# A decoder layer on one core: ScalarE normalises the attention's rows instead of VectorE, GpSimd makes the offsets, and the calls of all engines stand in another sequence

## The chip, the cores and the metric

The kernel runs on one core of a Trainium2 chip. A core has TensorE (PE, matrix products, with weight loads shown as PEld), VectorE (DVE), ScalarE (ACT, table functions and affine maps), GpSimd (POOL) and SyncE (SP), which here only issues transfers. Each engine works through its own list of instructions in order and waits at semaphores for the others. The metric is the device time of one execution in microseconds (us), lower is better.

## The reference, cut to what matters

```python
# x, ctx: (16, 256, 512); one decoder layer
Q = (LN(x) @ wq.T) in 16 heads of 32;  K, V = one shared head of 32, both squeezed to 8 and grown again
Q, K = rope(Q), rope(K);  K, V = quantise_8bit(K), quantise_8bit(V)      # over all 16 batches
for i in range(0, 256, 64):                                              # windows of 128 keys
    wout = (sigmoid(Qw Kw^T / sqrt(32)) / (row sum + 1e-8)) Vw           # blended where windows overlap
x1 = x + out @ wo.T
k  = LN(x1)                                                              # the step that is moved
x2 = x1 + wkv(w, u, k, ctx)                                              # a scan over 256 tokens
h  = silu(q(LN(x2)) @ tern(w_gate).T) * (q(LN(x2)) @ tern(w_up).T)
out = x2 + q(rms_norm(h) * ln_weight) @ tern(w_down).T                   # q: 8 bit per row, tern: -1, 0, 1
```

`LN` is `(x - mean) / sqrt(var + 1e-5)` over the 512 columns, without weights.

## The kernel before, in words

**Tiles.** A batch is 256 tokens by 512 columns: two halves `t` of 128 token rows (one per partition), or four chunks `c` of 128 columns. The hidden width 2048 is worked in four pieces `n` of 512. All arithmetic but the matrix products of the feed-forward part is fp32.

**Stages.** A long prologue brings in all of `x`, makes K and V of all batches, finds their common extrema and rounds the three weight matrices to -1, 0, 1. Then each batch passes through attention (`queries`, `rope`, `rotate`, `scores`, `probs`, `dens`, `nums`, `blend_windows`, `attention_out`, `residual`), the norm of its rows (`att_norm`), the scan (`key_steps`, `wkv_keys`, `exps`, `values`, `scan`, `join`, `outputs`, `quotient`, `wkv_back`, `wkv_residual`), quantisation (`wkv_norm`, `wkv_quantise`, `scale_tokens`, `wkv_round`) and the feed-forward part (`gate_up`, `silu`, `hidden`, `squares`, `weigh_hidden`, `peak`, `hidden_scale`, `scale_hidden`, `round_hidden`, `down`, `output`).

**What sets the order.** There is no scheduler. Each of the five engine programs is a list of calls written out by hand: a prologue, a loop `for i in range(4, B)` that is a software pipeline (batch `b = i` is in attention while `w = i-1` is in the scan and `f`, `g`, `h` = `i-2`, `i-3`, `i-4` are in the feed-forward part), and an epilogue. One pass of the loop is called a round here; it takes one batch in and one out. The lists differ in where a round is cut, which by itself means nothing: what counts is the sequence and the semaphores.

**The norm.** `residual` adds the attention's output to the rows of `x` and takes `bn_stats` of each half (L1425, L1427). `att_norm` (DVE) joins the statistics into mean and variance (L1376), waits for GpSimd's `att_rstd`, which adds epsilon and raises to the power -1/2 (L1805, L1807), and then subtracts the mean and multiplies by the inverse deviation in one `tensor_scalar` per half (L1381), from `x_rows` into `tok`. GpSimd's `key_steps` subtracts a table from `tok` (L1842), TensorE's `wkv_keys` transposes it (L618), ScalarE's `exps` (L1003) follows.

**The ways between the engines that the prediction walks.** `wkv_round` (L1504) writes the quantised tokens `q_tok`; SyncE's `turn_tokens` (L337) transposes them by a transfer into `qT`; TensorE's `gate_up` (L646) reads them and ScalarE's `silu` (L1012) reads its first result. `hidden_scale` (L1531 to L1537) releases `scale_hidden` (L986, the multiply) and `round_hidden` (L996, to bf16), two long ScalarE steps for each half of the hidden rows. `probs` (L947) is the sigmoid of the scores, sixteen pieces per batch, in four groups between which TensorE makes the next scores. `spin` (L658) is a run of products that nobody reads, put where TensorE would stand idle. Change of function set on ScalarE costs a load of its tables (rows with ACT_TABLE_LOAD): `silu`, `probs` and the logarithms and exponentials each need another set.

Of the kernel before, what the change touches and what calls it, by code (L numbers as in the profile page):

```python
# [13 lines left out]
P = 128  # L14
# [27 lines left out]
def build(nc, a, out, k_scratch, v_scratch):  # L42
# [10 lines left out]
    spare = sb("spare", [P, 1])  # L53
    warm = sb("warm", [P, 1])
# [155 lines left out]
    eps_set, win_set = event("eps_set", 6), event("win_set", 4)  # L210
# [29 lines left out]

    key_T, exp_set, value_set = event("key_T"), event("exp_set", NC), event("value_set")
# [24 lines left out]
    def sync_program(sy):  # L266
# [115 lines left out]
        load_x(0)  # L382
        load_small()
        load_x(1)
        load_columns(0)
        load_columns(2)
        load_columns(1)
        load_x(2)
        load_x(3)
        load_columns(3)  # L390
        load_x(4)
        load_columns(4)
        load_x(5)
        store_trig(1)
        load_columns(5)
        load_x(7)
        store_trig(0)
        load_columns(6)
        load_x(6)
        load_keys(0)  # L400
        load_wq()
        load_columns(7)
        load_weights(GATE, 1)
        load_weights(GATE, 0)
        load_queries(0)
        store_trig(5)
        load_weights(GATE, 2)
        next_residual(1)
        store_trig(2)
        load_weights(GATE, 3)  # L410
# [4 lines left out]
        next_keys(0)  # L415
        load_weights(UP, 2)
        load_weights(UP, 3)
        next_queries(0)
        next_residual(0)
        store_trig(3)  # L420
        load_weights(DOWN, 1)
        load_weights(DOWN, 0)
        turn_queries(1, 0)
        store_trig(4)
        load_weights(DOWN, 2)
        turn_queries(1, 1)
        store_trig(6)
        load_weights(DOWN, 3)
        store_trig(7)
        next_queries(1)  # L430
        next_keys(1)
        next_values(0)
        turn_tokens(0)
        turn_queries(2, 0)
        turn_queries(2, 1)
        next_queries(2)
        next_keys(2)
        next_values(1)
        turn_tokens(1)
        turn_hidden(0, 0, 0)  # L440
        turn_queries(3, 0)
        turn_queries(3, 1)
        turn_hidden(0, 0, 1)
        for i in range(4, B):
            b, w, f, g, h = i, i - 1, i - 2, i - 3, i - 4
            next_keys(w)
            next_queries(w)
            turn_hidden(h, 1, 0)
            turn_hidden(h, 1, 1)
            store(h, 1)  # L450
            store(h, 0)
            next_residual(f)
            next_values(f)
# [1329 lines left out]
    def pool_program(ge):  # L1783
# [35 lines left out]
        def att_rstd(b):  # L1819
            row_rstd("att", b, x1_mv, x1_var, x1_rstd)  # L1820
# [260 lines left out]
```

## Time and profile before

| | |
|---|---|
| median of 3 runs | 994.83 us (992.13 to 996.42) |
| the profiled execution's own time | 994.31 us |
| its span, first to last instruction | 992.2 us |
| TensorE busy | 886.7 us (89%) |
| VectorE busy | 818.8 us (83%) |
| ScalarE busy | 712.6 us (72%) |
| GpSimd busy | 429.3 us (43%) |
| TensorE's mean granted clock | 0.981 of full speed |

How to read it: 2.1 us of the time lie outside the span. All engines are on for most of the time, so a share says little; the chain of work that ended last has 41% TensorE, 17% VectorE, 14% ScalarE, 11% issue, 6% transfers, 5% GpSimd. Most of the span is rounds that repeat to within 0.1 us on every engine, so one round can be read step by step. In the rows, `idle before <-releaser` in brackets is how long the engine had stood still and what ended it; where none stands, it had not.

### The profile page before, as it was taken

The page shows a single profiled execution, that of the slowest core. Times are in us where ns is not written, and L with a number is a line of the kernel's source. Part 1 is how long each engine was busy: PE and PEld are TensorE (multiplying, and loading weights), DVE is VectorE, ACT ScalarE, POOL GpSimd, SP SyncE. Part 2 cuts the span into 40 slices and gives each one's busy share as a digit, 9 for nine tenths or more (in the row PEclk, how much of TensorE's full clock was granted, in tenths as well). Part 3 has the DMA queues.
Part 4 walks back from the last instruction along what each step waited for, and adds up shares of the span by engine and source line. Part 5 has one row for each costly group of instructions (what it writes and reads, how often), then busy time and mean ns, then how long its engine had stood idle before and what let it go on. Part 6 is the DMA issues. An engine that isn't in the chain of part 4 may idle for free.

```text
span 992.2 us, 22539 instructions
## 1 busy us (share of the span) xinstructions
PE 886.7 (89%) x8569; PEld 551.6 (56%) x8668; DVE 818.8 (83%) x1519; ACT 712.6 (72%) x1188; POOL 429.3 (43%) x510
## 2 busy tenths in 40 slices
PE   6998877889798989898989999999989898987897
PEld 3456564665465656565555565556555555653454
DVE  4677586998898989897989898979797989887953
ACT  1148283566879797978878887888888878796665
POOL 2111203454264536363646363736354544545532
PEclk9999898999999999999999999999999999998999
DMA  9988260201423232323161513343223333222023
GB/s 358 392 351 307 87 217 1 72 23 21 114 76 83 92 88 86 94 80 100 65 114 65 115 65 98 82 88 82 82 68 97 81 90 79 85 77 66 20 64 95
DMA packets 119387, 107.19 MB, mean 108 GB/s; under 512 B 91792, under 2 KB 94720, under 8 KB 118128
## 3 DMA queue, kind: packets, MB, share of 16 engines
q1 hardware_dynamic: 116320, 100.64, 34.5%
q10 hardware_dynamic: 2336, 2.52, 0.8%
q0 software_dynamic: 624, 2.59, 0.7%
q8 instruction: 68, 1.11, 0.5%
q14 instruction: 39, 0.32, 0.1%
HBM read 65.62 MB, written 10.75 MB: 77 GB/s over the span
## 4 chain that ended last, share of the span: by engine, by line
PE 41%; DVE 17%; ACT 14%; issue 11%; DMA 6%; POOL 5%; SPq 3%; DVEq 0%; ACTq 0%; POOLq 0%
PE bank L646 11%; PE bank L666 7%; PE bank L585 7%; PE bank L558 4%; PE bank L608 4%; PE bank L577 4%; ACT arena L947 3%; DMA work<-work 2%; DVE fs L1524 2%; ACT junk L1012 2%; ACT work L986 2%; POOL sums L1835 2%; DVE rows L1425 1%; PE bank L627 1%; DVE amax L1493 1%
## 5 line engine op out<-in xcount | busy, mean ns | idle before, releaser
L1852 POOL TENSOR_TENSOR work<-junk,lnw 128x512 f32<-128x512 f32 x128 | 175.2, 1387 | 183.8 <-DVE junk L1515 183.4
L646 PE MATMUL bank<-w_up_gate,qT 128*128 128x512 bf16 x967 | 226.8, 381 | 19.1 <-DMA qT<-q_tok 6.6
L646 PEld LDWEIGHTS bank<-w_up_gate,qT 128*128 128x128 bf16 x1024 | 95.4, 98 | 126.9 <-DMA qT<-q_tok 9.0
L947 ACT ACTIVATE arena<-bank 128x384 f32<-128x384 f32 x256 | 104.9, 496 | 33.9 <-PE bank L577 33.7
L666 PE MATMUL bank<-w_down,work 128*128 128x512 bf16 x470 | 111.8, 380 | 18.1 <-DMA work<-work 7.2
L1017 ACT ACTIVATE junk<-junk,deq 128x512 f32<-128x512 f32 x128 | 92.6, 723 | 42.7 <-DVE junk L1515 42.3
L558 PE MATMUL bank<-wide,wq_sb 128*128 128x256 f32 x512 | 117.2, 388 | 3.2 <-DVE rows L1425 3.2
L1515 DVE TENSOR_TENSOR junk<-bank,junk 128x512 f32<-128x512 f32 x128 | 84.9, 680 | 41.2 <-issue 25.4
L608 PE MATMUL bank<-wo_sb,wide 128*128 128x512 f32 x256 | 115.5, 605 | 1.4 <-DVE wide L1418 1.4
L558 PEld LDWEIGHTS bank<-wide,wq_sb 128*128 128x128 f32 x512 | 98.2, 194 | 26.9 <-issue 13.4
L986 ACT ACTIVATE work<-work,fs 128x2048 f32<-128x2048 f32 x32 | 64.0, 2001 | 67.7 <-DVE fs L1537 67.7
L1835 POOL TENSOR_TENSOR sums<-sums,blend 128x448 f32<-128x448 f32 x64 | 82.6, 1302 | 29.9 <-ACT sums L963 29.9
L1012 ACT ACTIVATE junk<-bank,deq 128x512 f32<-128x512 f32 x128 | 83.5, 680 | 8.5 <-PE bank L646 6.4
L577 PE MATMUL bank<-wide,k_win 32*128 32x128 f32 x1536 | 61.2, 288 | 29.0 <-ACT arena L947 18.1
L666 PEld LDWEIGHTS bank<-w_down,work 128*128 128x128 bf16 x512 | 45.8, 98 | 67.4 <-issue 8.1
L1448 DVE TENSOR_TENSOR_SCAN sums<-wkv_s,sums 128x256 f32<-128x256 f32 x128 | 79.2, 689 | 3.9 <-ACT sums L1003 3.9
L608 PEld LDWEIGHTS bank<-wo_sb,wide 128*128 128x128 f32 x256 | 49.6, 195 | 58.9 <-issue 55.4
L577 PEld LDWEIGHTS bank<-wide,k_win 32*128 32x128 f32 x1536 | 49.2, 186 | 56.2 <-ACT arena L947 36.7
L1524 DVE TENSOR_REDUCE fs<-work 128x1 f32<-128x2048 f32 x32 | 72.8, 2276 | 0.7 <-POOL work L1852 0.7
L658 PE MATMUL bank<-blend,ident 128*128 128x256 f32 x280 | 69.3, 392 | 3.6 <-ACT junk L1012 3.6
L1456 DVE SCALAR_TENSOR_TENSOR sums<-sums,wkv_s 128x512 f32<-128x512 f32 x64 | 66.3, 1094 | 0.0
L585 PE MATMUL bank<-arena,one_win 128*32 128x128 f32 x1536 | 55.8, 286 | 8.6 <-ACT arena L947 8.6
(154 smaller groups left out, 1565.3 us busy)
## 6 DMA issues: line engine op xcount, KB each, us to landing
sums<-in_xT SPq DMA_DIRECT2D x8, 1024.0 KB, 10.0
wide<-in_xT SPq DMA_DIRECT2D x16, 512.0 KB, 4.4
wide<-wide SPq DMA_DIRECT2D x64, 128.0 KB, 2.1
out<-rows SPq DMA_DIRECT2D x32, 256.0 KB, 2.1
rows<-in_x SPq DMA_DIRECT2D x15, 512.0 KB, 3.6
ctx_T<-in_ctxT SPq DMA_DIRECT2D x15, 512.0 KB, 4.5
kv_b<-k_raw SPq DMA_DIRECT2D x64, 96.0 KB, 2.2
work<-in_wgT SPq DMA_DIRECT2D x4, 1024.0 KB, 14.5
```

Of the source, the lines that this page charges most:

```text
L558: last = te.matmul(in_bank(k, 2)[:, n % 2, :], wq_sb[:, c, n * P:(n + 1) * P], xT[:, c, :], start=c == 0, stop=c == NC - 1)
L577: last = te.matmul(bank[j][:, n * P:(n + 1) * P], k_win[head, window], q_cos[head, c, window], start=True, stop=True, skip_group_check=True)
L585: te.matmul(bank[k][j * HD:(j + 1) * HD, n * P:(n + 1) * P], by(n), prob[:, n, QUAD * c + j, :], start=n == 0, stop=True, skip_group_check ...
L608: last = te.matmul(bank[t][:, :], heads_T[:, c, t * P:(t + 1) * P], wo_sb[:, c, :], start=c == 0, stop=c == NC - 1)
L646: last = te.matmul(bank[4 + k % 4][:, :], qT[:, c, t * P:(t + 1) * P], w_up_gate[:, m, c, cols], start=c == 0, stop=c == NC - 1)
L666: last = te.matmul(bank[6 + t][:, :], hid_T[:, t, c, :], w_down[:, c, :], start=c == 0, stop=c == NI - 1)
L947: se.activation(prob[:, :, QUAD * c + j, :], bank[j][:, 0:NW * P].rearrange("p (k q) -> p k q", k=NW), ACT.Sigmoid, scale=float(1.0 / np.s ...
L1012: se.activation(gated[:, n % 2, :], bank[4 + 2 * (n % 2)][:, :], ACT.Silu, scale=deq[:, 0, t:t + 1]).then_inc(silu_set.sem, 1)
L1017: se.activation(gated[:, n % 2, :], hid[:, n % 2, :], ACT.Square, scale=deq[:, 1, t:t + 1], accum_out=fs[:, t, n:n + 1]).then_inc(sq_set.s ...
L1524: ve.tensor_reduce(col[t]["am"], hid_w[:, t, :], AX.X, ALU.max, apply_absolute_value=True).then_inc(h_peak.sem, 1)
L1835: ge.tensor_tensor(soft[:, c, :], soft[:, c, :], blend[:, :], op=ALU.mult).then_inc(weighted.sem, 1)
L1852: ge.tensor_tensor(hid_w[:, t, cols], hid[:, n % 2, :], lnw[:, cols], op=ALU.mult).then_inc(z_set.sem, 1)
```

## The change

**The norm.** `att_norm` keeps only the join of the statistics. GpSimd's `att_rstd` makes, behind the inverse deviation, an offset per row: mean times inverse deviation, then zero minus that. A new ScalarE step `normalise_rows` forms `tok = rstd * x + offset` with one `activation` per half. A memset of the tile `zero` is added to the constants.

```diff
+    x1_off = sb("x1_off", [P, NT])
+    zero = sb("zero", [P, NT])
...
         def att_norm(b):
             row_stats("att", b, x1_bn, x1_mv)
-            ve.wait_ge(x1_rstd.sem, x1_rstd.at(b))
-            normalise("att", x_rows[b % 3], tok, x1_norm)
...
+        def normalise_rows(b):
+            st, mv, rs = stats["att"]
+            se.wait_ge(x1_moved.sem, x1_moved.at(b))
+            se.wait_ge(x1_bn.sem, x1_bn.at(b))
+            for t in range(NT):
+                se.activation(tok[:, t, :], x_rows[b % 3][:, t, :], ACT.Identity, scale=rs[:, t:t + 1],
+                              bias=x1_off[:, t:t + 1]).then_inc(x1_norm.sem, 1)
...
         def att_rstd(b):
             row_rstd("att", b, x1_mv, x1_var, x1_rstd)
+            st, mv, rs = stats["att"]
+            ge.wait_ge(x1_rstd.sem, x1_rstd.at(b))
+            if b:
+                ge.wait_ge(x1_norm.sem, x1_norm.at(b - 1))
+            ge.tensor_tensor(x1_off[:, :], mv[:, :, 0], rs[:, :], op=ALU.mult).then_inc(x1_moved.sem, 1)
+            ge.wait_ge(x1_moved.sem, x1_moved.at(b, 0))
+            ge.tensor_tensor(x1_off[:, :], zero[:, :], x1_off[:, :], op=ALU.subtract).then_inc(x1_moved.sem, 1)
```

**The sequences.** All five lists are written anew, prologue, loop and epilogue. Outside the loop the prediction speaks of two places, both on TensorE: in the prologue the spin ahead of `wkv_back(0, 0)` goes from `spin(0, 0, 3)` to `spin(0, 0, 15)`, and in the epilogue one goes away:

```diff
         gate_up(15, 1, 3)
-        spin(15, 16, 12)
         down(15, 0, 0)
```

In the loop, ScalarE's list between the first `silu` of a batch (the first row of the second block) and its first `probs`. The first block is the kernel before, from `scale_tokens` on; L980 is `scale_tokens`, L986 `scale_hidden` and L996 `round_hidden` of the second half of the hidden rows, L1012 `silu`, L1017 `squares`, L1003 `exps`:

```order
L980 ACTIVATE wide<-wide,amax 128x512 x2
L986 ACTIVATE work<-work,fs 128x2048
L996 ACTIVATE work<-work 128x2048
L1012 ACTIVATE junk<-bank,deq 128x512 x2
L951 ACT_TABLE_LOAD
L1017 ACTIVATE junk,fs<-junk,deq 128x512
L1003 ACTIVATE sums<-bank,wkv_s 128x256 x4
L1017 ACTIVATE junk,fs<-junk,deq 128x512
L1012 ACT_TABLE_LOAD
L1012 ACTIVATE junk<-bank,deq 128x512 x2
L947 ACT_TABLE_LOAD
```

The same place in the changed kernel; L1023 is `silu`, L1006 `normalise_rows`, L989 `scale_hidden`, L999 `round_hidden`, L1028 `squares`, L1014 `exps`:

```order
L1023 ACTIVATE junk<-bank,deq 128x512
L1006 ACTIVATE wide<-rows,x_off,rstd_att 128x512 x2
L989 ACTIVATE work<-work,fs 128x2048
L1023 ACTIVATE junk<-bank,deq 128x512
L954 ACT_TABLE_LOAD
L1028 ACTIVATE junk,fs<-junk,deq 128x512
L1014 ACTIVATE sums<-bank,wkv_s 128x256 x4
L1028 ACTIVATE junk,fs<-junk,deq 128x512
L999 ACTIVATE work<-work 128x2048
L1023 ACT_TABLE_LOAD
L1023 ACTIVATE junk<-bank,deq 128x512 x2
L950 ACT_TABLE_LOAD
```

`scale_hidden` and `round_hidden` of the second half stood ahead of the first `silu` and now stand behind it, and the two new activations stand there too. The number of table loads in a round stays five.

TensorE from the attention's last products (L608, L613) to the first scores (L577, L582), before. L558 is `queries`, L646 `gate_up`, L618 `wkv_keys`, L658 `spin`:

```order
L608 MATMUL bank<-wo_sb,wide 128x512 x8
L558 MATMUL bank<-wide,wq_sb 128x256 x16
L646 MATMUL bank<-w_up_gate,qT 128x512 x16
L618 MATMUL bank<-ident,wide 128x128 x8
L658 MATMUL bank<-blend,ident 128x256 x2
L646 MATMUL bank<-w_up_gate,qT 128x512 x16
L577 MATMUL bank<-wide,k_win 128x128 x12
```

And changed, L563 `queries`, L651 `gate_up`, L663 `spin`, L623 `wkv_keys`:

```order
L613 MATMUL bank<-wo_sb,wide 128x512 x8
L563 MATMUL bank<-wide,wq_sb 128x256 x8
L651 MATMUL bank<-w_up_gate,qT 128x512 x16
L663 MATMUL bank<-blend,ident 128x256 x2
L623 MATMUL bank<-ident,wide 128x128 x8
L563 MATMUL bank<-wide,wq_sb 128x256 x8
L651 MATMUL bank<-w_up_gate,qT 128x512 x16
L582 MATMUL bank<-wide,k_win 128x128 x12
```

Half of the queries has gone behind the transposes, so the first `gate_up` comes half a `queries` earlier. Behind the first scores there is a further `spin` of two products. Of the two `gate_up` calls that stood among the `nums`, one has gone ahead of the first `dens` and one behind the last `nums`.

VectorE behind `wkv_quantise`, before. L1425 and L1427 are `residual`, L1522 and L1524 `peak` of the second half, L1504 `wkv_round`, L1531 to L1537 `hidden_scale`, L1376 and L1381 `att_norm`:

```order
L1425 TENSOR_TENSOR rows<-bank,rows 128x512
L1427 BN_STATS stats_att<-rows 128x6
L1522 TENSOR_REDUCE fs<-fs 128x1
L1524 TENSOR_REDUCE fs<-work 128x1
L1504 TENSOR_SCALAR q_tok<-wide 128x512 x2
L1531 TENSOR_SCALAR fs<-fs 128x1
L1533 RECIPROCAL fs<-fs 128x1
L1534 TENSOR_SCALAR fs<-fs,w_mean 128x1
L1537 TENSOR_SCALAR fs<-fs 128x1
L1374 MEMSET spare 128x1
L1376 BN_AGGR mv_att<-stats_att 128x2 x2
L1381 TENSOR_SCALAR wide<-rows,mv_att,rstd_att 128x512 x2
```

And changed, L1519 `wkv_round`, L1393 the join of the statistics, L1537 and L1539 `peak`, L1546 to L1552 `hidden_scale`:

```order
L1442 TENSOR_TENSOR rows<-bank,rows 128x512
L1444 BN_STATS stats_att<-rows 128x6
L1519 TENSOR_SCALAR q_tok<-wide 128x512 x2
L1391 MEMSET spare 128x1
L1393 BN_AGGR mv_att<-stats_att 128x2 x2
L1537 TENSOR_REDUCE fs<-fs 128x1
L1539 TENSOR_REDUCE fs<-work 128x1
L1546 TENSOR_SCALAR fs<-fs 128x1
L1548 RECIPROCAL fs<-fs 128x1
L1549 TENSOR_SCALAR fs<-fs,w_mean 128x1
L1552 TENSOR_SCALAR fs<-fs 128x1
```

The rounding of the tokens and the join of the statistics have gone ahead of the long reduction of `peak`; the two `tensor_scalar` are gone. GpSimd does, in this order, the inverse deviation of `hidden_rstd` (which needs the first row of `peak`), `wkv_steps`, `att_rstd` with the offsets and `key_steps`; it did so before.

## Rows read from the trace of the kernel before

**Rows 1.** Busy time of each engine, its share of the span, instructions.
```profile
PE 886.7 (89%) x8569; PEld 551.6 (56%) x8668; DVE 818.8 (83%) x1519; ACT 712.6 (72%) x1188; POOL 429.3 (43%) x510
```

**Rows 2.** Stretches: us, busy (instructions) per engine, TensorE clock, DMA share, GB/s.
```profile
340.76:391.73 50.97, 47.52 (x510) 29.65 (x516) 45.38 (x85) 42.28 (x71) 25.64 (x30) 1.00 0.31 87
...
854.11:909.05 54.94, 48.06 (x511) 29.38 (x516) 47.86 (x88) 42.03 (x70) 26.84 (x34) 1.00 0.25 63
...
289.79:909.05 619.26, 571.33 (x6110) 355.36 (x6192) 549.14 (x1012) 504.26 (x840) 309.35 (x364) 1.00 0.32 85
```

**Rows 3.** Timeline of VectorE in one round: start, us, what, [idle before].
```profile
540.15 0.69 DVE L1515 TENSOR_TENSOR junk<-bank,junk 128x512 f32<-128x512 f32 x1
...
548.72 0.14 DVE L1522 TENSOR_REDUCE fs<-fs 128x1 f32<-128x4 f32 x1
...
550.97 0.75 DVE L1504 TENSOR_SCALAR q_tok<-wide 128x512 bf16<-128x512 f32 x2
...
553.67 1.00 DVE L1381 TENSOR_SCALAR wide<-rows,mv_att,rstd_att 128x512 f32<-128x512 f32 x2 [1.10 <-POOL rstd_att L1807]
...
591.12 0.69 DVE L1515 TENSOR_TENSOR junk<-bank,junk 128x512 f32<-128x512 f32 x1
```

**Rows 4.** Timeline of ScalarE in the same round.
```profile
552.50 2.00 ACT L986 ACTIVATE work<-work,fs 128x2048 f32<-128x2048 f32 x1 [3.69 <-DVE fs L1537]
554.53 1.91 ACT L996 ACTIVATE work<-work 128x2048 bf16<-128x2048 f32 x1
556.35 1.25 ACT L1012 ACTIVATE junk<-bank,deq 128x512 f32<-128x512 f32 x2
...
565.77 1.64 ACT L947 ACTIVATE arena<-bank 128x384 f32<-128x384 f32 x4
```

**Rows 5.** Timeline of TensorE in the same round.
```profile
539.95 7.03 PE L608 MATMUL bank<-wo_sb,wide 128*128 128x512 f32 x16
546.91 7.14 PE L558 MATMUL bank<-wide,wq_sb 128*128 128x256 f32 x32
554.11 3.40 PE L646 MATMUL bank<-w_up_gate,qT 128*128 128x512 bf16 x15
...
567.47 0.95 PE L577 MATMUL bank<-wide,k_win 32*128 32x128 f32 x24 [1.05 <-ACT arena L947]
...
574.40 0.86 PE L585 MATMUL bank<-arena,one_win 128*32 128x128 f32 x24 [0.56 <-ACT arena L947]
```

**Rows 6.** Timeline of GpSimd in the same round.
```profile
548.94 0.19 POOL L1869 TENSOR_TENSOR fs<-fs,per_row 128x1 f32<-128x1 f32 x1 [5.55 <-DVE fs L1522]
...
550.46 0.20 POOL L1863 TENSOR_TENSOR deq<-amax,w_mean 128x4 f32<-128x4 f32 x1 [0.17 <-POOL fs L1877]
...
552.65 0.19 POOL L1805 TENSOR_TENSOR rstd_att<-mv_att,ln_eps 128x2 f32<-128x2 f32 x1 [1.99 <-DVE mv_att L1376]
...
584.34 1.30 POOL L1883 TENSOR_TENSOR sums<-sums 128x512 f32<-128x512 f32 x1
```

**Rows 7.** ScalarE, groups by line and shape: xcount, busy, mean ns.
```profile
L980 ACT ACTIVATE wide<-wide,amax 128x512 f32<-128x512 f32 x32 | 21.2, 709 | 20.2 <-DVE amax L1497 20.2
L936 ACT ACTIVATE k_win<-kv_b,grid 128x256 f32<-128x256 f32 x16 | 9.6, 601 | 0.4
L930 ACT ACTIVATE v_win<-kv_b,grid 128x96 f32<-128x96 f32 x16 | 7.3, 455 | 0.0
```

**Rows 8.** TensorE in prologue and epilogue, where it had stood idle or spun.
```profile
161.12 1.94 PE L627 MATMUL bank<-ident,sums 128*128 128x128 f32 x8 [5.24 <-DVE sums L1416]
162.85 9.20 PE L608 MATMUL bank<-wo_sb,wide 128*128 128x512 f32 x16
...
910.31 2.64 PE L646 MATMUL bank<-w_up_gate,qT 128*128 128x512 bf16 x8 [4.20 <-DMA qT<-q_tok]
...
973.42 5.34 PE L658 MATMUL bank<-blend,ident 128*128 128x256 f32 x24
980.06 1.67 PE L666 MATMUL bank<-w_down,work 128*128 128x512 bf16 x7 [1.29 <-DMA work<-work]
```

More of the change, by code:

```diff
@@ L824, in tensor_program @@
             scores(b, 3)
-        gate_up(13, 1, 0)
-        dens(15, 0)
-        dens(15, 1)
-        dens(15, 2)
-        down(12, 1, 1)
-        nums(15, 0)
-        dens(15, 3)
-        nums(15, 1)
-        nums(15, 2)
+            gate_up(f, 1, 0)
+            dens(b, 0)
+            down(g, 1, 1)
+            dens(b, 1)
+            dens(b, 2)
+            nums(b, 0)
+            dens(b, 3)
+            nums(b, 1)
+            nums(b, 2)
+            nums(b, 3)
         gate_up(13, 1, 1)
-        nums(15, 3)
         gate_up(13, 1, 2)
-        gate_up(13, 1, 3)
         wkv_back(14, 0)
         wkv_back(14, 1)
+        gate_up(13, 1, 3)
         attention_out(15, 0)
         attention_out(15, 1)
+        spin(13, 16, 10)
         gate_up(14, 0, 0)
@@ L854, in tensor_program @@
         gate_up(14, 1, 1)
[L855 removed]
         wkv_back(15, 0)
         wkv_back(15, 1)
+        gate_up(14, 1, 2)
         gate_up(14, 1, 3)
[L859 removed]
+        spin(14, 16, 17)
         gate_up(15, 0, 0)
@@ L1650, in vector_program @@
         wkv_residual(1, 1)
-        hidden(0, 1, 1)
+        hidden(0, 1, 2)
         wkv_norm(1)
-        hidden(0, 1, 2)
         hidden_scale(0, 0)
         wkv_quantise(1)
+        hidden(0, 1, 3)
         residual(2)
-        wkv_round(1)
-        hidden(0, 1, 3)
-        att_norm(2)
-        peak(0, 1)
-        hidden(1, 0, 0)
-        hidden_scale(0, 1)
-        hidden(1, 0, 1)
-        rope(3, 0)
         for i in range(4, B):
             b, w, f, g, h = i, i - 1, i - 2, i - 3, i - 4
+            wkv_round(g)
+            att_norm(f)
+            peak(h, 1)
+            hidden_scale(h, 1)
+            hidden(g, 0, 0)
+            rope(w, 0)
+            hidden(g, 0, 1)
             rope(w, 1)
+            rotate(w, 0)
+            scan(f, 0)
             values(f)
-            rotate(w, 0)
             rotate(w, 1)
-            scan(f, 0)
             scan(f, 1)
@@ L1697, in vector_program @@
             residual(w)
-            peak(g, 1)
-            wkv_round(f)
-            hidden_scale(g, 1)
-            att_norm(w)
-            hidden(f, 0, 0)
-            hidden(f, 0, 1)
-            rope(b, 0)
+        wkv_round(13)
+        att_norm(14)
+        peak(12, 1)
+        hidden_scale(12, 1)
+        hidden(13, 0, 0)
+        hidden(13, 0, 1)
+        rope(15, 0)
         rope(15, 1)
```

560 lines of the change are left out of this document (283 added, 277 removed).

## The prediction, on record before the result

> **What bounds the kernel now.** I read four views in this order: the busy times, the windows, the chain of waits and the timelines of one round.
>
> The busy times show TensorE at 89%, VectorE at 83% and ScalarE at 72% [rows 1]. That is too close together to name a bound. The windows show that 289.79 to 909.05 us, 62% of the span, is twelve rounds, and that a clean round takes 50.97 us with TensorE busy for 47.52, VectorE for 45.38 and ScalarE for 42.28 [rows 2]. No engine fills the round, so its length is set by a loop of waits that runs through several of them. A round can be cut at any event, so I cut it at two. H is the start of the batch's last `hidden` on VectorE, 540.15, which comes again at 591.12, 50.97 later [rows 3]. P is the start of `probs` on ScalarE, 565.77 [rows 4]. So H to P takes 25.62 us and P to the next H 25.35.
>
> *H to P.* VectorE works without a gap worth naming to the end of `residual`, where the first row of `peak` starts at 548.72, H+8.6; `peak` and `wkv_round` follow, the latter at 550.97, H+10.8 [rows 3]. ScalarE waits 3.69 us for `hidden_scale`, then does `scale_hidden` and `round_hidden` of the second half, and reaches `silu` at 556.35, H+16.2. From there to P it is never idle: 9.42 us [rows 4]. TensorE's queries take 7.14 us and end at 554.05, and `gate_up` starts at 554.11 [rows 5]. The transposed tokens thus arrive when TensorE is ready for them.
>
> *P to H.* ScalarE's sigmoids alternate with TensorE's scores, where TensorE waits 1.05 and 0.56 us [rows 5]. Then the logarithms and exponentials go to GpSimd, which does the two middle windows, `outputs` and the last window; `outputs` starts at 584.34 with no idle time before it [rows 6], and VectorE's blends, quotient and residual behind it lead to H.
>
> **The change, part by part.**
>
> *VectorE loses work.* A round loses the two L1381 (1.00 us) and the wait of 1.10 us before them [rows 3]. In the place where that stood, VectorE next waits for the transposes and for `gate_up`, so the 2.1 us bring nothing by themselves. What is late next is the first `gate_up`.
>
> *GpSimd gains two small operations.* The nearest rows are a `tensor_tensor` of one column, 0.19 us, and of four, 0.20 us [rows 6]; two in a row, each waiting for the one before, come to about 0.5 us per round. At worst all of it shifts `normalise_rows`, at best none. `wkv_round` and the join of the statistics end by H+9.7 in the new order. From the first row of `peak` to the end of `wkv_steps` is 1.94 us (548.72 to 550.66), from `att_rstd` to what it releases 1.02 (552.65 to 553.67), and the offsets take 0.5 [rows 3, 6]: with a few hand-overs the activations could start at H+13.3. That is when the first `silu` ends (below), so I charge nothing.
>
> *ScalarE gains two activations.* No row has this form. L980 has one operand per partition and takes 0.709 us at 512 columns. L936 and L930 have two, as the new one has: 0.601 us at 256 columns and 0.455 at 96 [rows 7], a slope of 0.91 ns a column, which gives 0.83 at 512. Between 0.71 and 0.83 I take 0.80; consecutive ones overlap by 0.1, so a pair costs 1.5 us (1.3 to 1.55). The Trainium skill (ScalarE: Activation LUTs, section What ACT_TABLE_LOAD costs) says that each such operand adds about 93 ns; for one operand at 512 columns its figures give 706 ns, with which the trace agrees at 709, and for two an estimate of 0.80 us. That speaks against moving this step to ScalarE: the pair takes half as long again as VectorE's 1.00.
>
> *The new H to P.* `wkv_round` no longer waits behind `peak`: it starts at H+8.6. From its start to the first product on its result took 3.14 us (550.97 to 554.11); TensorE was then only just free, so it can be a few tenths less. `gate_up` starts at H+11.7. TensorE is free from H+10.3 (6.76 us to the end of L608, and half of the 7.14 us) and waits 1.4 us [rows 5]. Four of the sixteen products (0.85 us) and a hand-over of 0.1 release `silu` at H+12.65, which is 3.5 us earlier than before. But behind this `silu` now stands more than the 9.42 us of before: `scale_hidden` (2.03, 552.50 to 554.53), `round_hidden` (1.82, to 556.35) and the two new activations (1.5), 5.35 together [rows 4]. None of it can run ahead of `silu`, because ScalarE works in order. So P comes at 12.65 + 9.42 + 5.35 = H+27.4, 1.8 us later than now. Put otherwise: ScalarE's idle time between H and P stays about what it was, and the 1.5 us of new work come on top of it. TensorE's own way to the first scores (four `gate_up`, a spin, the transposes and half of the queries, some 12.7 us from H+11.7) ends near H+24.5, in time for P.
>
> *The new P to H.* The second spin (1.0 us) goes into the gap of 1.05 us before the second scores, and `gate_up` into the gap of 0.56 us before `dens` [rows 5]. TensorE comes to `wkv_back` about 0.8 us earlier relative to P. But ScalarE has the same nine activations before the second exponential as now, GpSimd's `outputs` stands behind the same windows, and the blend that frees the bank stays where it was, so H follows P by 25.35 us as before. Bounds: 0.5 less, if GpSimd's chain is looser than I read it, or 0.5 more.
>
> *The rounds.* 27.4 + 25.35 = 52.8 us against 50.97. For the eleven rounds up to 854.11 that is 11 x 1.8 = +20 us (+12 to +26 with the bounds of the activation, of the transfer and of the way P to H).
>
> *The two ends.* All else in the prologue I cost at nothing: its loads, keys and weight roundings are in another order but the same. One term I take: TensorE stood idle for 5.24 us before `wkv_back(0)` and then did L608 in 9.20 us, against 7.03 in a round [rows 5, 8]; fifteen spins fill that, so -3 us. From 854.11 to the end: the last round took 54.94 us in the old epilogue's order [rows 2]; the loop's order now reaches it (-2), and the last batch's scan starts earlier, which I leave within the bounds. Against that, the spin of 5.34 us before the last products is gone. TensorE then stands still from 973.4 to 980.1; after 4.20 us of idle time eight products took 2.64 us [rows 8], nearly twice the 0.21 us each that seven in 1.67 us show, so the last 32 products can cost up to 6.8 us more; most of them wait for transfers anyway, and I take +1.5. Ends together: -3.5 (-10 to +6).
>
> *Sum.* 20 - 3.5 = +16.5 us on the profiled execution's 994.31 (span 992.2 and 2.1 outside it) gives 1010.8; the median is 0.5 above that execution, within the spread. I say **1010 us**.
>
> **Rivals.**
>
> *VectorE's time comes back (faster).* If the loop of waits is really tied to VectorE, 45.38 us busy, each round can lose up to 2.1 us, and TensorE's floor of 47.52 + 1.0 for the new spin allows it. For it: VectorE has almost no idle time between H+18 and the next H. Against it: the piece before that waits for others. At the full 2.1 the result is 994 - 25 - 3 = 966, at a fifth of it 986; I give this case 980.
>
> *The new work hides (no change).* If `silu` starts early enough, or `scale_hidden` fits into the wait, the 1.5 us go into the 3.69 us of ScalarE's idle time [rows 4] and the rounds stay at 51; only the ends move: 991. Against it is that `scale_hidden` now stands behind `silu`, not in that wait.
>
> *The clock falls in the rounds (much slower).* TensorE would wait 1.4 us more at one place. If it then ran the next 7 us of products at the lower level, each round would lose about 5 us: 1065. Against it: it stood at 1.00 in the rounds with gaps of 1.05 us [rows 2, 5], and the falls came behind idle times of 4 and 5 us [rows 8].
>
> *The edit does not do what it says.* It does: the two activations stand in ScalarE's list once a batch, and table loads stay at five a round.
>
> **How the numbers follow.** Forecast 0.67; VectorE's time back 0.17; hidden 0.11; clock 0.05. The forecast's own range is 1000 to 1020. To reach eight in ten the range goes down to the edge of the hidden case and up past the forecast's bounds: 990 to 1024. A measurement of this kernel tells 0.5%, about 5 us, from no change. Faster by more: 0.17. Within: 0.11. Slower: 0.67 + 0.05 = 0.72.
>
> **What the new profile would show.** Right: rounds of about 52.8 us; ScalarE without idle time from the first `silu` of a batch to `probs`, 14.8 us instead of 9.4; a wait of 1 to 2 us before the first `gate_up`, ended by the transfer; the new activations at 0.80 us; VectorE busy for 44.4 us a round, with more idle time than now before `rope`. Wrong: rounds below 51 us; a transfer under 2.5 us with `silu` at H+11.9 or earlier; P to H shorter than 24.8 us; or prologue and epilogue that differ from now by more than 10 us together.

## The result and the profile after

The changed kernel takes 1004.52 us (median of 8 runs, 999.75 to 1010.76), the kernel before beside it 993.92 (8 runs, 992.13 to 996.42): a ratio of 1.0118, with a 95% interval of 1.0097 to 1.0139. It is slower, as forecast, by 10.6 us where I had said 16. The profiled execution is the shortest of the eight, 999.75 us with a span of 998.3, so all that is read from its trace stands against a difference of 5.4 us (6.1 in the span).

Busy times and stretches of the changed kernel, to be read against [rows 1, 2]:

```profile
PE 892.5 (89%) x8625; PEld 553.7 (55%) x8700; DVE 792.4 (79%) x1488; ACT 737.3 (74%) x1223; POOL 435.9 (44%) x542
```

```profile
601.68:653.97 52.29, 48.88 (x516) 30.23 (x520) 44.18 (x82) 43.38 (x73) 25.83 (x32) 1.00 0.31 85
863.55:915.73 52.18, 48.81 (x517) 30.56 (x522) 43.86 (x79) 43.38 (x73) 26.51 (x33) 1.00 0.28 67
```

The mark of a batch, used from here on, is the start of its first `bn_stats`, 6.6 us behind H; 601.68 and 863.55 are such marks. A round takes 52.3 us instead of 50.97, the last one 52.18 instead of 54.94. VectorE is busy for 44.2 us of a round instead of 45.4, ScalarE for 43.4 instead of 42.3; the clock stays at 1.00.

VectorE in one round (start, us, what, idle before and what ended it). L1530 is `hidden`, the first and last row are H; L1519 is `wkv_round`, L1418 `rope`, L1424 `rotate`:

```profile
595.06 0.68 DVE L1530 TENSOR_TENSOR junk<-bank,junk 128x512 f32<-128x512 f32 x1
...
603.61 0.74 DVE L1519 TENSOR_SCALAR q_tok<-wide 128x512 bf16<-128x512 f32 x2
...
608.32 0.69 DVE L1530 TENSOR_TENSOR junk<-bank,junk 128x512 f32<-128x512 f32 x1 [0.76 <-PE bank L651]
612.26 1.29 DVE L1418 TENSOR_TENSOR wide<-bank,kv_b 128x512 f32<-128x512 f32 x2 [3.24 <-PE bank L623]
...
615.81 1.29 DVE L1418 TENSOR_TENSOR wide<-bank,kv_b 128x512 f32<-128x512 f32 x2 [1.67 <-PE bank L563]
618.43 0.69 DVE L1424 TENSOR_TENSOR wide<-wide 128x512 f32<-128x512 f32 x1 [1.34 <-DMA wide<-wide]
...
647.35 0.68 DVE L1530 TENSOR_TENSOR junk<-bank,junk 128x512 f32<-128x512 f32 x1
```

ScalarE, then TensorE, then GpSimd in the same round. L1023 is `silu`, L1006 the new `normalise_rows`, L950 `probs` (its row is P); L651 is `gate_up`, L663 the spin, L563 the second half of the queries; L1840 the first offset operation, L1864 `key_steps`:

```profile
607.54 0.69 ACT L1023 ACTIVATE junk<-bank,deq 128x512 f32<-128x512 f32 x1 [2.28 <-PE bank L651]
608.13 1.51 ACT L1006 ACTIVATE wide<-rows,x_off,rstd_att 128x512 f32<-128x512 f32 x2
...
622.07 1.64 ACT L950 ACTIVATE arena<-bank 128x384 f32<-128x384 f32 x4
```

```profile
606.61 3.40 PE L651 MATMUL bank<-w_up_gate,qT 128*128 128x512 bf16 x15 [1.13 <-DMA qT<-q_tok]
609.85 1.03 PE L663 MATMUL bank<-blend,ident 128*128 128x256 f32 x4
...
612.05 3.62 PE L563 MATMUL bank<-wide,wq_sb 128*128 128x256 f32 x16
```

```profile
607.37 0.19 POOL L1840 TENSOR_TENSOR x_off<-mv_att,rstd_att 128x2 f32<-128x2 f32 x1
...
609.01 2.50 POOL L1864 TENSOR_TENSOR wide<-wide,grow_tab 128x512 f32<-128x512 f32 x2 [1.17 <-ACT wide L1006]
```

Every step between H and P is where I had put it: `wkv_round` at H+8.55 (forecast 8.6), `gate_up` at H+11.55 after 1.13 us of waiting for the transfer (11.7 and 1.4), `silu` at H+12.48 (12.65), the pair of activations 1.51 us (1.5), ScalarE without a gap from there to P for 14.53 us (14.8), P at H+27.01 (27.4), and the next H 25.28 later (25.35). All the signs I had named for "right" are there. The experiments show that this is only a part of the cause, and the rows above already hold another: VectorE stands idle four times between H+12.5 and H+23.4, the last time for the transfer before `rotate` at 618.43, and then not at all until the next H, 28.92 us later.

### The profile page after: what moved, and what is told of

It reads as the page before. It is cut to its first block, busy times and chain, and to the rows that moved or that the text cites. A ratio compares the mean times of both kernels' runs of the same rounds, so it can differ in the third digit from the quotient of the medians.

```text
span 998.3 us, 22694 instructions
## 1 busy us (share of the span) xinstructions
PE 892.5 (89%) x8625; PEld 553.7 (55%) x8700; DVE 792.4 (79%) x1488; ACT 737.3 (74%) x1223; POOL 435.9 (44%) x542
## 3 DMA queue, kind: packets, MB, share of 16 engines
q8 instruction: 69, 1.13, 0.5%
## 4 chain that ended last, share of the span: by engine, by line
ACT 25%; issue 19%; DVE 17%; PE 16%; POOL 11%; DMA 5%; SPq 1%; DVEq 0%; ACTq 0%; POOLq 0%
PE bank L671 5%; ACT arena L950 4%; PE bank L582 4%; DMA qT<-q_tok 3%; POOL sums L1857 3%; ACT work L989 3%; DVE junk L1530 3%; POOL work L1874 2%; PE bank L651 2%; POOL sums L1905 2%; ACT junk L1023 2%; ACT L954 2%; ACT junk L1028 2%; DVE rows L1442 2%; DVE amax L1508 2%
## 5 line engine op out<-in xcount | busy, mean ns | idle before, releaser
L651 PE MATMUL bank<-w_up_gate,qT 128*128 128x512 bf16 x966 | 225.5, 379 | 24.1 <-DMA qT<-q_tok 16.1
L651 PEld LDWEIGHTS bank<-w_up_gate,qT 128*128 128x128 bf16 x1024 | 95.6, 98 | 132.8 <-DMA qT<-q_tok 18.9
L671 PE MATMUL bank<-w_down,work 128*128 128x512 bf16 x495 | 118.7, 384 | 21.7 <-ACT junk L1023 9.1
L950 ACT ACTIVATE arena<-bank 128x384 f32<-128x384 f32 x256 | 104.9, 498 | 31.8 <-PE bank L582 31.6
L1028 ACT ACTIVATE junk<-junk,deq 128x512 f32<-128x512 f32 x128 | 92.6, 724 | 32.6 <-DVE junk L1530 32.1
L563 PE MATMUL bank<-wide,wq_sb 128*128 128x256 f32 x512 | 116.2, 381 | 0.0
L613 PE MATMUL bank<-wo_sb,wide 128*128 128x512 f32 x256 | 113.6, 597 | 0.0
L1023 ACT ACTIVATE junk<-bank,deq 128x512 f32<-128x512 f32 x128 | 84.3, 680 | 34.9 <-PE bank L651 34.0
L563 PEld LDWEIGHTS bank<-wide,wq_sb 128*128 128x128 f32 x512 | 95.3, 190 | 22.8 <-issue 10.9
L1530 DVE TENSOR_TENSOR junk<-bank,junk 128x512 f32<-128x512 f32 x128 | 84.7, 678 | 24.7 <-PE bank L651 14.5
L1418 DVE TENSOR_TENSOR wide<-bank,kv_b 128x512 f32<-128x512 f32 x64 | 41.1, 685 | 68.1 <-PE bank L623 45.9
L989 ACT ACTIVATE work<-work,fs 128x2048 f32<-128x2048 f32 x32 | 63.9, 1996 | 35.4 <-DVE fs L1552 33.2
L613 PEld LDWEIGHTS bank<-wo_sb,wide 128*128 128x128 f32 x256 | 49.1, 192 | 56.4 <-issue 54.3
L663 PE MATMUL bank<-blend,ident 128*128 128x256 f32 x312 | 77.2, 389 | 0.4 <-ACT junk L1023 0.4
L582 PE MATMUL bank<-wide,k_win 32*128 32x128 f32 x1536 | 61.8, 290 | 15.4 <-ACT arena L950 9.5
L582 PEld LDWEIGHTS bank<-wide,k_win 32*128 32x128 f32 x1536 | 49.9, 188 | 42.0 <-ACT arena L950 28.0
L1539 DVE TENSOR_REDUCE fs<-work 128x1 f32<-128x2048 f32 x32 | 72.8, 2275 | 0.3 <-POOL work L1874 0.3
```

The costliest lines, as they stand in the source:

```text
L563: last = te.matmul(in_bank(k, 2)[:, n % 2, :], wq_sb[:, c, n * P:(n + 1) * P], xT[:, c, :], start=c == 0, stop=c == NC - 1)
L582: last = te.matmul(bank[j][:, n * P:(n + 1) * P], k_win[head, window], q_cos[head, c, window], start=True, stop=True, skip_group_check=True)
L613: last = te.matmul(bank[t][:, :], heads_T[:, c, t * P:(t + 1) * P], wo_sb[:, c, :], start=c == 0, stop=c == NC - 1)
L651: last = te.matmul(bank[4 + k % 4][:, :], qT[:, c, t * P:(t + 1) * P], w_up_gate[:, m, c, cols], start=c == 0, stop=c == NC - 1)
L671: last = te.matmul(bank[6 + t][:, :], hid_T[:, t, c, :], w_down[:, c, :], start=c == 0, stop=c == NI - 1)
L950: se.activation(prob[:, :, QUAD * c + j, :], bank[j][:, 0:NW * P].rearrange("p (k q) -> p k q", k=NW), ACT.Sigmoid, scale=float(1.0 / np.s ...
```

## The experiments

All of them are built on one substitution: the two kinds of transfer that turn the tokens and the hidden rows copy the same bytes to the same tiles unturned. The feed-forward part then works on unturned data. So the kernel before and the changed one were run in that form too, as bases. The kernel before ran beside them all as it is, and each ratio is to that.

Two theories. **A** is that of the prediction: ScalarE's list between the first `silu` and `probs` sets P, and the next H follows P by 25.3 us. **D**, formed after the runs with the edit undone and with the edit alone: a round is the way from H to the last `rotate` for which VectorE waits, called R here, and behind it VectorE's block of work, in which it has no idle time up to the next H. B (VectorE's load as a whole) and C (TensorE and the transfer) are the rivals in the texts on record.

**The bases.**

> The base of the following runs: the kernel before, in which the two kinds of transfer that turn the tokens and the hidden rows copy the same bytes to the same tiles without turning them (so the feed-forward part works on unturned data and its result is another). Both theories: a plain transfer takes about the time of a turning one (2.4 us for the tokens, 3.5 us for half of a hidden row block, perhaps 0.3 to 1 us less). In the kernel before TensorE is only just free when the tokens land, so a round stays within 0.3 us of 50.97 and the whole within 5 us of 994.

> The base again, for its time beside the other kernels of this call: the kernel before with plain transfers, 989 us in one look.

> The changed kernel with the same plain transfers as the base (989 us in one look). Theory A (ScalarE's list between the first silu and probs sets the way H to P): what the transfer gains moves the first gate_up and silu forward by up to 0.3 us, so rounds of 52.0 to 52.3; the ratio to the base of the kernel before stays at 1.01, so about 999 us.

```diff
-                sy.dma_start(qT[:, :, t * P:(t + 1) * P], q_tok[:, t, :], transpose=True)
+                sy.dma_start(qT[:, :, t * P:(t + 1) * P], q_tok[:, t, :].rearrange("p (c q) -> p c q", q=P))
...
-            sy.dma_start(hid_T[:, t, half, :], hid_q[:, t, k * I // 2:(k + 1) * I // 2], transpose=True)
+            sy.dma_start(hid_T[:, t, half, :], hid_q[:, t, k * I // 2:(k + 1) * I // 2].rearrange("p (c q) -> p c q", q=P))
```

The kernel before in this form takes 989.11 us in a single run and 991.53 as the median of 12 (ratio 0.9983, 0.9968 to 0.9997), the changed one 1000.58 (1.0070, 1.0046 to 1.0095). Clean rounds are 50.97 and 52.3 us as with the turning transfers, so the bases stand for the two kernels. The difference of 9.0 us is what is to be explained. Since the feed-forward part's result is another in this form, these kernels serve for times only.

**The edit undone in the new sequences.**

> The changed kernel's sequences (with plain transfers), but VectorE normalises again (two tensor_scalar right behind hidden_scale of the second half), no activations and no offsets. Theory A: the list is 1.5 us shorter, silu starts as before at H+12.5, P moves from H+27.0 to H+25.5, a round from 52.3 to 50.8 us; twelve rounds give 18 us: 1.8% less than the changed kernel, so a little under the kernel before. Theory B (VectorE's load sets the round): VectorE gets 1.0 us more, rounds 53.3, 12 us above the changed kernel. Theory C (the new sequences on TensorE and the transfer behind wkv_round set it, not ScalarE's list): rounds as in the changed kernel.

```diff
+        def att_rows(b):
+            ve.wait_ge(x1_rstd.sem, x1_rstd.at(b))
+            normalise("att", x_rows[b % 3], tok, x1_norm)
...
             peak(h, 1)
             hidden_scale(h, 1)
+            att_rows(f)
...
-            normalise_rows(w)
```

1006.18 us, ratio 1.0135 (1.0103 to 1.0167): not 18 us less than the changed base but 5.6 more. Between the same two batches (b = 3 and 14, eleven rounds) it takes 575.9 us, the changed base 575.3: rounds of 52.35 and 52.30. Theory A asked for 50.8. VectorE's and ScalarE's rows of one round; L1520 is `hidden`, L1410 `rotate`, L949 `probs`:

```profile
602.25 0.68 DVE L1520 TENSOR_TENSOR junk<-bank,junk 128x512 f32<-128x512 f32 x1
...
625.19 0.69 DVE L1410 TENSOR_TENSOR wide<-wide 128x512 f32<-128x512 f32 x1 [1.30 <-DMA wide<-wide]
```

```profile
627.01 1.28 ACT L949 ACT_TABLE_LOAD   x1 [0.40 <-PE bank L581]
628.30 1.64 ACT L949 ACTIVATE arena<-bank 128x384 f32<-128x384 f32 x4
```

The next H is at 654.66. P did come earlier, at H+26.05 instead of H+27.1, and even waited for the scores; but then H came 26.36 us after P, not 25.3. So P alone does not set the next H, and A as it stands falls. R came 0.51 us earlier too (H+22.94 for 23.45), and the block behind it was 0.52 us longer; D says nothing of that, and why it is so comes behind the table. B falls as well: VectorE does 45.6 us in this round and 44.2 in the changed base's, and the rounds are equal.

**The edit alone in the old sequences.**

> The kernel before (with plain transfers) with the edit alone: ScalarE normalises right behind round_hidden of the second half, GpSimd makes the offsets, all sequences as before. Theory A: the two activations stand where ScalarE is never idle on the way to P: P from H+25.6 to H+27.1, a round from 51.0 to 52.5, 1.8% above the base. Theory B: VectorE loses 2.1 us of a round with its wait: rounds of 49 to 50.5, 0.5 to 2.4% under the base. Theory C: the activations fit into ScalarE's idle time, no difference.

```diff
             round_hidden(g, 1)
+            normalise_rows(w)
```

1019.24 us, ratio 1.0267 (1.0241 to 1.0292), 27.7 us above its base instead of 18. Eleven rounds take 586.6 us against 562.7, 2.17 each. C falls for this sequence, and B too, since VectorE has 1.0 us less to do in a round (44.4 for 45.4). The rows of a round in which H is 659.39 (L1006 `normalise_rows`, L621 the transposes, L1418 `rope`, L1424 `rotate`):

```profile
675.59 1.50 ACT L1006 ACTIVATE wide<-rows,x_off,rstd_att 128x512 f32<-128x512 f32 x2
```

```profile
677.88 0.63 PE L621 MATMUL bank<-ident,wide 128*128 128x128 f32 x4 [1.13 <-POOL wide L1864]
```

```profile
679.71 2.48 DVE L1418 TENSOR_TENSOR wide<-bank,kv_b 128x512 f32<-128x512 f32 x4 [0.67 <-PE bank L621]
...
684.93 0.69 DVE L1424 TENSOR_TENSOR wide<-wide 128x512 f32<-128x512 f32 x1 [0.56 <-DMA wide<-wide]
```

Where VectorE normalised at 654.01, ahead of ScalarE's long list (H is 640.49 in that round), the activations now stand at its end. `key_steps`, the transposes, `rope`, the transfer and `rotate` follow one on the other, and R moves from H+23.49 to H+25.54, by 2.05, in a round that is 2.0 longer. P moves as well, by 1.78, from H+25.62 to H+27.40, so this run alone tells little between A and D. In five of the eleven rounds the block is 0.5 to 0.9 us longer besides (27.97 to 28.29 us for 27.43).

**A round of the kernel before that was longer by itself.** In the kernel before, in its base and in the run with the new ends one round, that of b = 6 to 7, takes 52.7 to 52.9 us instead of 50.97; it is in the trace that I predicted from (442.69 to 495.55). Here in the base, VectorE, then ScalarE:

```profile
434.54 0.69 DVE L1515 TENSOR_TENSOR junk<-bank,junk 128x512 f32<-128x512 f32 x1
...
459.46 0.69 DVE L1407 TENSOR_TENSOR wide<-wide 128x512 f32<-128x512 f32 x1 [1.96 <-DMA wide<-wide]
...
487.43 0.68 DVE L1515 TENSOR_TENSOR junk<-bank,junk 128x512 f32<-128x512 f32 x1
```

```profile
460.16 1.64 ACT L947 ACTIVATE arena<-bank 128x384 f32<-128x384 f32 x4
```

P is at H+25.62, to the hundredth where it is in a clean round. R is 1.43 us late, because the transfer is, and the next H is 1.92 late. In the trace that I predicted from P is 0.22 us late in that round, R 1.42 and the next H 1.90. Such a round shows without any experiment that H does not follow P by a fixed time, and the prediction did not read it.

**Two tests of D, made after it was formed.**

> The changed kernel (plain transfers) with two calls moved in the loop: on GpSimd att_rstd with the offsets ahead of hidden_rstd of the second half, on ScalarE normalise_rows ahead of the first silu. ScalarE then normalises in its wait of 2.3 us, silu starts 0.5 us later and P comes 0.9 us earlier; key_steps ends 1.0 us earlier, but TensorE's spin before wkv_keys ends as before, so wkv_keys and the second half of the queries gain only the 0.25 to 0.35 us that TensorE waited for GpSimd. Theory A (P sets the next H): rounds of 51.4, 1000.6 to about 990. Theory D (the queries' second half, the transfer of 2.7 us behind it and VectorE's unbroken block of 28.95 us from the first rotate to H set the round): rounds of 52.0, about 997.

```diff
-            hidden_rstd(g, 1)
-            wkv_steps(f)
             att_rstd(w)
+            hidden_rstd(g, 1)
+            wkv_steps(f)
             key_steps(w)
...
-            silu(f, 0, 0)
             normalise_rows(w)
+            silu(f, 0, 0)
```

> As the run before, and without the spin of two products (0.86 us) that stands before wkv_keys in the loop. ScalarE's list is the same as there. Theory A: nothing more, rounds as in the run before. Theory D: wkv_keys and the second half of the queries come 1.1 us earlier than in the changed kernel, the first rotate too, rounds of 51.3, about 989; if P, 0.9 us earlier, is then the later of the two, 51.4.

```diff
             gate_up(f, 0, 1)
-            spin(f, 4, 2)
             wkv_keys(w)
```

The first takes 997.76 us (1.0037, 1.0019 to 1.0055) with rounds of 52.31, the second 985.22 (0.9907, 0.9874 to 0.9940) with rounds of 51.24. In both P is the same to 0.1 us, at H+26.02 and H+25.95. Theory A gives both the same time, 11 us under the changed base; the first gained nothing in its rounds, the second 1.06 us in each. TensorE and VectorE in the first (H 597.84), then in the second (H 589.45):

```profile
612.62 1.03 PE L663 MATMUL bank<-blend,ident 128*128 128x256 f32 x4
613.48 1.04 PE L623 MATMUL bank<-ident,wide 128*128 128x128 f32 x8
614.36 3.62 PE L563 MATMUL bank<-wide,wq_sb 128*128 128x256 f32 x16
```

```profile
620.75 0.69 DVE L1424 TENSOR_TENSOR wide<-wide 128x512 f32<-128x512 f32 x1 [1.35 <-DMA wide<-wide]
```

```profile
604.25 1.11 PE L623 MATMUL bank<-ident,wide 128*128 128x128 f32 x8
605.19 3.62 PE L563 MATMUL bank<-wide,wq_sb 128*128 128x256 f32 x16
```

```profile
611.54 0.69 DVE L1423 TENSOR_TENSOR wide<-wide 128x512 f32<-128x512 f32 x1 [1.31 <-DMA wide<-wide]
```

In the second `gate_up` takes over from the queries at 608.65, and R follows 2.9 us later, when the transfer has landed. A spin of two products, meant to fill a gap, stood on the path for its full 0.86 us. For the rounds D had said 52.0 and 51.3, A 51.4 for both. The first lies nearer to D, 0.3 above it. The second by itself tells nothing, since it is also P plus 25.3; what tells is that taking the spin away left P where it was and took 1.07 us from the round. In one table, with each round's length, from the start of H to the next:

| kernel | H to R | R to H | round | H to P |
|---|---|---|---|---|
| before (base) | 23.49 | 27.47 | 50.96 | 25.62 |
| before (base), the long round | 24.92 | 27.97 | 52.89 | 25.62 |
| edit alone, old sequences | 25.54 | 27.42 | 52.96 | 27.40 |
| changed (base) | 23.45 | 28.95 | 52.40 | 27.08 |
| new sequences, VectorE normalises | 22.94 | 29.47 | 52.41 | 26.05 |
| changed, norm early | 22.91 | 29.53 | 52.44 | 26.02 |
| changed, norm early, no spin | 22.09 | 29.16 | 51.25 | 25.95 |

P alone does not order the rounds: 1.03 us of P between rows 4 and 5 are worth nothing, and rows 6 and 7 differ by 1.2 us at the same P. Nor does R alone: its 0.51 us between rows 4 and 5 are worth nothing either. (The old loop's R is its second `rotate`, with the product of `values` and the other `rotate` done before it; the new loop's is the first, so its block is 1.5 us longer for the same work.)

**How P acts on VectorE's block.** The block has no idle time, but its operations differ in length: `refine` and the quotient take 0.68 us each at their shortest. Here are, for the kernel before, GpSimd's first `outputs` and first `weigh_windows` (L1883, L1835) and VectorE's first quotient (L1469), then `outputs` and the pair of `refine` in the changed base (L1905, L1477), then the same two in the run without the spin (L1904, L1476):

```profile
578.25 1.20 POOL L1883 TENSOR_TENSOR sums<-sums 128x512 f32<-128x512 f32 x1 [0.27 <-ACT sums L973]
579.70 1.31 POOL L1835 TENSOR_TENSOR sums<-sums,blend 128x448 f32<-128x448 f32 x1 [0.25 <-ACT sums L963]
580.03 1.52 DVE L1469 SCALAR_TENSOR_TENSOR sums<-sums 128x512 f32<-128x512 f32 x1
```

```profile
632.72 1.19 POOL L1905 TENSOR_TENSOR sums<-sums 128x512 f32<-128x512 f32 x1
633.38 1.68 DVE L1477 TENSOR_TENSOR sums<-sums 128x512 f32<-128x512 f32 x2
```

```profile
627.87 1.19 POOL L1904 TENSOR_TENSOR sums<-sums 128x512 f32<-128x512 f32 x1 [0.24 <-ACT sums L975]
628.30 1.91 DVE L1476 TENSOR_TENSOR sums<-sums 128x512 f32<-128x512 f32 x2
```

The quotient takes 1.52 us and ends 0.54 us behind `weigh_windows` (581.01). Of the pair of `refine` the second takes 0.68 us, but the first 1.08 in the changed base and 1.30 without the spin, and it ends 0.55 and 0.54 us behind `outputs`. `outputs` starts 12.47 or 12.48 us behind P in all three: in the first and the last it is released by ScalarE, whose list runs on from P, and in the changed base GpSimd's work before it ends just then. So there is a way from P over ScalarE, GpSimd and a held-up VectorE operation to H, and it takes 25.3 us: nine of the base's eleven rounds have 25.34 or 25.35 from P to H, the changed base's eleven 25.29 to 25.38, the eleven without the spin 25.29 or 25.30.

In rows 5 and 6 P is a good 1 us earlier than in row 4 and R only 0.5. `outputs` then starts 12.93 us behind P, held up by GpSimd's own steps behind VectorE's `peak`; the first `refine` takes 1.02 us, and the second starts 0.15 us behind `weigh_windows` (P+14.44) and takes 1.64. The pair takes 2.58 us for 1.68, the second quotient 0.68 for 1.02, together 0.56 more, which is about what R had gained.

Two ways thus lead to H, one over P and one over R, and in the changed kernel they end together. The rounds got shorter only in the run that moved both (rows 4 and 7: P by 1.13 us, R by 1.36, the round by 1.15). This is read from the rows: no run moved R alone, and none moved GpSimd's operations alone.

A rival that none of the texts names is TensorE's load, 48.9 us of a round in the changed base for 47.5 in the base, 1.4 more where the round is 1.4 longer. But with the edit alone it is 47.9 and the round 2.1 us longer, TensorE still has 3.5 us of idle time in the changed base's round, and between R and H VectorE shows no wait for it.

**The new ends on the old loop.**

> The kernel before (plain transfers, VectorE normalises) with its own prologue and loop, and behind the loop the changed kernel's sequences on all five engines, the last round in the loop's order. From 851 us to the end the base takes 139.0 us and the changed kernel 133.8 from the same mark: if that is the order's doing alone and not that of ScalarE's norm, this kernel is 4 to 5 us faster than the base, 987. If it hangs on the norm on ScalarE, no gain.

```diff
+        gate_up(13, 1, 3)
         attention_out(15, 0)
         attention_out(15, 1)
+        spin(13, 16, 10)
         gate_up(14, 0, 0)
...
         gate_up(15, 1, 3)
-        spin(15, 16, 12)
         down(15, 0, 0)
```

987.43 us, ratio 0.9939 (0.9915 to 0.9963), 4.1 under the base's median. Its trace, from an execution that took 992.93, shows less: from the mark of b = 14 to the end 137.3 us against 139.0 in the base and 133.8 in the changed base. The last round is shorter by 3.1 us (51.85 for 54.98) and the rest longer by 1.4. So the order gives a gain of about half a per cent by the medians; whether 1.7 or 4 us of it are the order's, the two intervals, which only just part, don't tell.

The version without the spin is faster than both kernels, 0.93% under the kernel before (0.60 to 1.26). It was measured with plain transfers only; the base with plain transfers has a median of 991.53 us, against which it is 6.3 us, 0.6%.

## Why the prediction was right, and where its reason was wrong

**The sum.** The forecast was +20 for the rounds and -3.5 for the ends. The eleven rounds up to the mark of b = 14 take 576.04 us after and 564.32 before: +11.7. Prologue and end give -2.3 and -3.3, together -5.6. That is +6.1 in the profiled span. Of the 8 us by which the rounds were forecast too long, 11 x 0.4 are the difference between the 52.8 I gave and 52.37, and the rest is that I took 50.97 for every round of before, whose mean is 51.30; the long round above and some smaller ones are gone in the new sequence. The steps that mis-sized it are "So P comes at 12.65 + 9.42 + 5.35 = H+27.4", 0.4 too late, and "11 x 1.8 = +20 us", which takes the clean round for the mean of before.

**H to P.** Right to 0.4 us in every number, as told above. The price of the pair was right too:

```profile
L1006 ACT ACTIVATE wide<-rows,x_off,rstd_att 128x512 f32<-128x512 f32 x32 | 24.1, 803 | 22.6 <-POOL x_off L1842 22.6
```

803 ns against 0.80 worked out. Offsets on GpSimd ended at 607.83, before `silu` had ended, and cost nothing here.

**P to H.** Here the reason was half of the truth: "the blend that frees the bank stays where it was, so H follows P by 25.35 us as before". In this kernel it does, by 25.28, and the way over GpSimd told above explains how. But the new sequences with VectorE's norm have P 1.03 us earlier, the same round, and 26.36 us from P to H. The step took the way over P for the only one and left out the one over R. I had read the block behind P as ScalarE's and GpSimd's because its first waits were theirs, and the prediction itself noted that VectorE has almost none between H+18 and the next H.

**TensorE's half of the queries.** "TensorE's own way to the first scores (...) ends near H+24.5, in time for P": I checked the moved half of `queries` against the scores alone. It has a nearer reader. `rope` needs it, the transfer of `turn_queries` waits for `rope` and for both halves of the queries, and `rotate` needs the transfer. Before, the queries ended at H+13.9, before the first `gate_up`, and R was set by the transposes. After, they end near H+20.6, behind `gate_up`, the spin and the transposes, and set R. The two `rope` halves and `rotate` wait for 3.24, 1.67 and 1.34 us. By this way the round is 1.3 us longer, since the block behind R, at an unmoved R, holds 1.5 us more work. By the way over P it is so too: P is 1.4 us later. Whether one of the two would have been enough isn't shown; no run put the queries back by themselves.

**The two parts of the change by themselves.** I forecast the cost as that of the edit: 1.5 us of new work on ScalarE, and gains elsewhere that about cancel. The medians of the four kernels say otherwise: sequences alone +14.7 us (1006.18 for 991.53), edit alone +27.7, both together +9.0. In the old sequences the edit costs 2.2 us a round, in the new ones none: rounds of 52.30 with it, 52.35 without. There it sets P 1.03 us and R 0.51 us later, and the block is as much shorter as R is later. The 5.6 us between the medians therefore lie outside the rounds: the two single traces, 11.1 us apart, have 8.4 in the prologue (b = 3 at 286.2 us against 294.6) and 2.3 at the end (133.8 against 136.1). How much of that the edit gives isn't shown, since the prologue differs by up to 4.5 us between kernels that have the same one (below). The forecast gave the rounds' loss wholly to the edit's 1.5 us and charged TensorE's reordering at nothing, while the sequences alone lose as much. That the sum came out near all the same is luck.

**The ends.** "fifteen spins fill that, so -3 us" failed. TensorE in the prologue, and behind the last `gate_up`:

```profile
153.91 6.74 PE L663 MATMUL bank<-blend,ident 128*128 128x256 f32 x30
166.41 1.97 PE L632 MATMUL bank<-ident,sums 128*128 128x128 f32 x8 [5.76 <-DVE sums L1484]
168.17 8.19 PE L613 MATMUL bank<-wo_sb,wide 128*128 128x512 f32 x16
...
985.98 1.86 PE L671 MATMUL bank<-w_down,work 128*128 128x512 bf16 x4 [6.78 <-DMA work<-work]
988.06 3.35 PE L671 MATMUL bank<-w_down,work 128*128 128x512 bf16 x11 [0.22 <-issue]
991.83 3.61 PE L671 MATMUL bank<-w_down,work 128*128 128x512 bf16 x16 [0.41 <-DMA work<-work]
```

The spins run out 5.76 us before `wkv_back(0)` can start; before, the wait was 5.24 [rows 8]. L613 gained 1 us (8.19 for 9.20), still short of 7.03. The prologue's 2.3 us can't be credited to anything: three kernels with one and the same prologue (changed base, norm early, no spin) reach b = 3 at 286.2, 290.7 and 288.7 us. Without the final spin TensorE waited 6.78 us and the first four products took 0.47 us each, the last sixteen 0.23; yet the stretch behind the last mark is 82.57 us for 83.15, so the +1.5 I took for it doesn't show in the sum; other calls in it have moved as well, and what the spin does there isn't shown. I had also misread its price: seven products in 1.67 us are 0.24 each, not 0.21, and the 0.33 of the slow eight is 1.4 times that, not nearly twice.

**The rivals.** "VectorE's time comes back" had the right engine and the wrong place: the norm stood in the part of the round where VectorE waits in any case (it is idle for some 8 us of a round after the change), so that a gift of 2.1 us there is worth nothing; the same in its block was not tried. "The new work hides" is what the edit does in the rounds of the new sequences, though not in the wait of 3.69 us that I named. "The clock falls" did not come: 1.00 in the rounds with a wait of 1.13 us each. Its price of 5 us a round stands in no row; the slow stretch of [rows 8] cost 2.2 us (9.20 for 7.03).

**What stays open.** How much slack ScalarE's list has in the changed kernel was not tried by adding to it. By the way over P it should have none, and GpSimd's third `weigh_windows` ends only 0.14 us before VectorE's blend needs it. Nor were the prologue's and the last spin run by themselves. Why the transfer of one round comes 1.4 us late in the old loop isn't shown.

## What to carry to other kernels

Look for the engine that works without a break for half of the round, and cut the loop where its last wait ends as well as at the event that looks central. Work given to or taken from it ahead of that wait was worth nothing here unless it moved what ends the wait. Then see whether the operations in the unbroken stretch are longer than their shortest, and beside what: a stretch without idle time can still be held up. Where two ways end together, taking time from one is worth nothing, which is no proof that the other is the cause. When a call is moved, follow its nearest reader on every engine, not the reader that seemed to matter; and a spin or filler is free only if nothing behind it is awaited. Before choosing between two loops of waits, look for a round that is longer by itself and see which event moved with it; and name signs that only one of the rivals would show, since all of mine came true under half a cause.

## What the runs showed of the hardware that I had not expected

**VectorE's operations are held up beside GpSimd's.** The same quotient (L1484, L1474) took 1.02 us in the changed base and 0.68 in the kernel with VectorE's norm. VectorE and GpSimd in the changed base, then in the other:

```profile
640.85 1.02 DVE L1484 SCALAR_TENSOR_TENSOR sums<-sums 128x512 f32<-128x512 f32 x1
```

```profile
640.08 1.25 POOL L1857 TENSOR_TENSOR sums<-sums,blend 128x448 f32<-128x448 f32 x1
```

```profile
650.31 0.68 DVE L1474 SCALAR_TENSOR_TENSOR sums<-sums 128x512 f32<-128x512 f32 x1
```

```profile
641.23 1.19 POOL L1893 TENSOR_TENSOR sums<-sums 128x512 f32<-128x512 f32 x1
...
648.33 1.24 POOL L1845 TENSOR_TENSOR sums<-sums,blend 128x448 f32<-128x448 f32 x1
```

Where GpSimd's operation had ended at 649.57 the quotient took 0.68 us; where one ran to 641.33 it took 1.02. The pair of `refine` goes the other way: 1.68 us in the changed base, where the second starts in GpSimd's pause (633.91 to 634.69), and 2.58 from 641.95 in the other, beside `outputs` and `weigh_windows`. The Trainium skill (SBUF — State Buffer, section "SBUF: two separate sides") says that a VectorE operation with two inputs in SBUF and a GpSimd operation that reads SBUF hold a shared port in turn, the second blocked until the first is done. The traces agree in kind: in all seven cases that I worked out (three quotients and four `refine`, in four kernels) the VectorE operation was 0.98 to 1.64 us long and ended 0.54 or 0.55 us behind GpSimd's, where the whole 0.68 behind it would be a little more. So a block that starts 0.5 us earlier against GpSimd's work can be 0.5 us longer. With the norm early R is 0.54 us earlier and the block 0.58 longer, of which `refine` and the quotient make 0.55.

**For the tokens a plain transfer takes as long as a turning one.** In the kernel before it is 2.3 us from issue to landing, plain, against 2.4. For half a block of hidden rows the medians over the whole run are 2.6 against 3.5, in the changed kernel 2.4 against 3.2; between 300 and 850 us they are 4.1 against 4.2 and 2.4 against 3.2.
